# Block-diagonals of B by a select on GpSimd from a ScalarE copy, in place of products on VectorE

## The reference

```python
x = conv(in_proj(ctx)); u = silu(x + conv_b)          # 256 channels, 256 tokens
dt_low, Bm, Cm = split(x_proj(u), [8, 8 + 16])        # Bm, Cm: 16 states per token
d = softplus(dt_proj(dt_low) + dt_proj_b)
def step(state, inp):                                 # d, b, c, u of one token
    state = state * exp(d[..., None] * A) + (d * u)[..., None] * b[:, None, :]
    return state, einsum('bdn,bn->bd', state, c)
y = (scan(step) + D * u) * silu(layernorm(x_in))
x = x_in + tanh(g_xattn) * y
out = x + tanh(g_ffn) * ffn(layernorm(x))             # quantized up, relu^2 gate, rmsnorm, quantized down
```

## Time and profile before

| | us |
|---|---|
| device time, median of 3 runs | 235.77 (234.69 to 237.27) |
| device time of the profiled execution | 236.09 |
| span of the profiled execution, first to last instruction | 234.3 |
| PE busy | 208.6 (89%) |
| DVE busy | 201.1 (86%) |
| POOL busy | 141.0 (60%) |
| ACT busy | 139.2 (59%) |

### The profile page before, as it was taken

How to read it: one execution, slowest core, us unless ns; L and a number is a source line. 1 busy time by engine, 2 the same in 40 slices (tenths; PEclk the granted TensorE clock), 3 DMA queues, 4 the chain that set the end, 5 groups by cost and what they waited for, 6 DMA issues and landing times.

```text
span 234.3 us, 3448 instructions
## 1 busy us (share of the span) xinstructions
PE 208.6 (89%) x1142; PEld 164.8 (70%) x1142; DVE 201.1 (86%) x299; ACT 139.2 (59%) x352; POOL 141.0 (60%) x98
## 2 busy tenths in 40 slices
...
DMA packets 9808, 14.01 MB, mean 60 GB/s; under 512 B 2520, under 2 KB 7360, under 8 KB 9792
## 3 DMA queue, kind: packets, MB, share of 16 engines
...
## 4 chain that ended last, share of the span: by engine, by line
PE 65%; DVE 23%; issue 6%; POOL 2%; ACT 2%; DVEq 0%; POOLq 0%
PE m_ps L910 20%; PE y_ps L932 17%; PE w_ps L961 10%; DVE bd L674 5%; PE w_ps L978 4%; DVE hb L729 3%; POOL hb L354 2%; PE w_ps L863 2%; DVE xc L658 2%; PE y_ps L832 2%; PE w_ps L879 1%; PE w_ps L987 1%; PE w_ps L871 1%; PE w_ps L885 1%; DVE xn L753 1%
## 5 line engine op out<-in xcount | busy, mean ns | idle before, releaser
L354 POOL TENSOR_TENSOR hb<-hb,cs 128x1024 f32<-128x1024 f32 x31 | 73.9, 2395 | 27.5 <-DVE hb L729 26.9
L729 DVE TENSOR_TENSOR_SCAN hb<-dA,m_ps 128x1024 f32<-128x1024 f32 x32 | 72.5, 2278 | 6.2 <-PE m_ps L910 5.5
L562 ACT ACTIVATE dA<-dt,nega 128x255 f32<-128x255 f32 (+1 forms) x160 | 59.4, 455 | 17.2 <-DVE hb L729 10.3
L910 PE MATMUL m_ps<-bd,duT 128*128 128x256 f32 (+1 forms) x224 | 63.9, 433 | 4.5 <-issue 3.8
L932 PE MATMUL y_ps<-hb,identf 128*128 128x256 f32 (+1 forms) x320 | 59.6, 339 | 0.7 <-POOL hb L354 0.6
L932 PEld LDWEIGHTS y_ps<-hb,identf 128*128 128x128 f32 x320 | 51.0, 191 | 6.7 <-POOL hb L354 1.4
L910 PEld LDWEIGHTS m_ps<-bd,duT 128*128 128x128 f32 x224 | 44.0, 202 | 16.5 <-issue 9.5
L961 PE MATMUL w_ps<-w13T,xqT 128*128 128x352 bf16 x192 | 30.6, 313 | 0.6 <-ACT xqT L583 0.5
L961 PEld LDWEIGHTS w_ps<-w13T,xqT 128*128 128x128 bf16 x192 | 18.5, 98 | 11.8 <-issue 1.6
L588 ACT ACTIVATE ru<-w_ps,finv 128x352 f32<-128x352 f32 x16 | 8.8, 548 | 20.3 <-PE w_ps L961 20.3
L674 DVE TENSOR_TENSOR bd<-identf,w_ps 128x1024 f32<-128x1024 f32 x16 | 18.7, 1213 | 1.4 <-PE w_ps L885 1.4
...
## 6 DMA issues: line engine op xcount, KB each, us to landing
...
```

The costliest lines, as they stand in the source:

```text
L354: E.tensor_tensor(h_g, h_g, cs[:, s0:s0 + sn, l0:l0 + ln], ALU.mult).then_inc(hc_end if (b, i, h) == OUT_END else hc_ok[h], 1)
L562: last = act_fn(dA_g[:, s, 1:ln], dt[:, p, h, l0 + 1:l0 + ln], ACT.Exp, scale=nega[:, h, s0 + s:s0 + s + 1])
L729: V.tensor_tensor_scan(hb[:, k % 3, h], dA[:, k % 2, h].rearrange("p n l -> p (n l)"), m_ps[:, h], 0.0, ALU.mult, ALU.add).then_inc(scan_o ...
L910: last = T.matmul(m_q[:, :, c * P - l0:(c + 1) * P - l0], duT[:, p, c, h * P:(h + 1) * P], bd[:, r, c, n0 + sn // 2 * q:n0 + sn // 2 * (q ...
```

## The change

A new step `bts` on ACT copies the transposed B (128 x 32) from PSUM to SBUF, once for each batch. The step `bd` moves from DVE to POOL, where two `affine_select` instructions read that copy, spread over 128 columns with stride 0, and keep it on the diagonal. PE makes one `bT` for each batch instead of two (four in all are gone: `bT/0.1`, `1.1`, `2.1`, `3.1`). `mix` waits for `bd_ok` alone. `relu` gets one wait more, for the `iqT` of two batches before.

```diff
@@ FILLS
-    "bT": [("bd", "dve")], "duT": [("duT", "act")],
+    "bT": [("bts", "act")], "duT": [("duT", "act")],
@@ build
         bd = sb("bd", [P, 2, HALVES, NS // 2, P])
+        bts = sb("bts", [P, 2, HALVES, NS])
@@ gpsimd
+                elif name == "bd":
+                    pool.wait_ge(free["act"], emptied("bT", b, 0))
+                    if b:
+                        pool.wait_ge(m_full, HALVES * (NG * (b - 1) + NG // 2 * (i + 1)))
+                    for c in range(HALVES):
+                        nc.gpsimd.affine_select(
+                            out=bd[:, i, c], in_=bts[:, p, c, NS // 2 * i:NS // 2 * (i + 1)].unsqueeze(2)
+                            .broadcast_to([P, NS // 2, P]), compare_op=ALU.is_equal, fill=0.0, base=0,
+                            pattern=[[0, NS // 2], [-1, P]], channel_multiplier=1).then_inc(bd_ok, 1)
@@ scalar
+                elif name == "bts":
+                    act.wait_ge(work_full, full("bT", b, 0))
+                    if b >= 2:
+                        act.wait_ge(bd_ok, 2 * HALVES * (b - 1))
+                    act_fn(bts[:, p].rearrange("p c n -> p (c n)"), bank("bT", b, 0)[:, 0:HALVES * NS],
+                           ACT.Copy).then_inc(free["act"], 1)
                 elif name == "relu":
                     h, c = i // 2, i % 2
                     act.wait_ge(work_full, full("up", b, i, 0))
+                    if b >= 2:
+                        act.wait_ge(work_full, full("iqT", b - 2, h, 1))
@@ vector
-                elif name == "bd":
-                    dve.wait_ge(work_full, full("bT", b, i))
-                    if b:
-                        dve.wait_ge(m_full, HALVES * (NG * (b - 1) + NG // 2 * (i + 1)))
-                    for c in range(HALVES):
-                        V.tensor_tensor(bd[:, i, c], identf[:, :].unsqueeze(1).broadcast_to([P, NS // 2, P]),
-                                        bank("bT", b, i)[:, c * NS + NS // 2 * i:c * NS + NS // 2 * (i + 1)]
-                                        .unsqueeze(2).broadcast_to([P, NS // 2, P]),
-                                        ALU.mult).then_inc(free["dve"] if c == HALVES - 1 else bd_ok, 1)
@@ tensor
-                        if c < HALVES - 1:
-                            pe.wait_ge(bd_ok, 2 * b + r + 1)
-                        else:
-                            pe.wait_ge(free["dve"], emptied("bT", b, r))
+                        pe.wait_ge(bd_ok, HALVES * (2 * b + r) + c + 1)
```

The orders of PE, ACT, DVE and POOL in `PLAN` are all written anew; two lines of it (POOL's first):

```diff
-        w_res/0.0 w_res/0.1 w_res/0.2 w_lo/0.0 w_lo/0.1 diag/0.0 w_lo/0.2 cubic/0.0 w_res/0.3 dtadd/0.0 w_lo/0.3
...
+        w_res/0.0 w_res/0.1 w_lo/0.0 w_lo/0.1 diag/0.0 w_res/0.2 bd/0.0 w_lo/0.2 bd/0.1 w_res/0.3 z/0.0 cubic/0.0
...
```

More of the change, by code:

```diff
@@ L53 @@
-        sum1/1.1 dtproj/2.0 bT/2.0 xqT/0.0 mix0/1.3 mix1/1.3 up/0.0 bT/2.1 sum0/1.2 sum1/1.2 duT/2.0 sum0/1.3
-        mix0/2.0 sum1/1.3 mix1/2.0 yT/1.0 skip/2.0 mix0/2.1 up/0.1 mix1/2.1 mix0/2.2 sum0/2.0 sum1/2.0 mix1/2.2
-        up/0.2 sum0/2.1 sum1/2.1 up/0.3 mix0/2.3 mix1/2.3 xqT/1.0 xdbl/3.0 up/1.0 dtproj/3.0 bT/3.0 bT/3.1 sum0/2.2
-        sum1/2.2 sum0/2.3 sum1/2.3 up/1.1 duT/3.0 up/1.2 mix0/3.0 up/1.3 mix1/3.0 mix0/3.1 iqT/0.0 yT/2.0 skip/3.0
-        sum0/3.0 mix1/3.1 down/0.0 mix0/3.2 sum1/3.0 sum0/3.1 iqT/0.1 sum1/3.1 xqT/2.0 mix1/3.2 down/0.1 mix0/3.3
@@ L58 @@
-        up/2.0 iqT/1.0 up/2.1 up/2.2 up/2.3 mix1/3.3 skip/3.1 yT/3.0 iqT/1.1 sum0/3.2 sum1/3.2 down/1.0 down/1.1
-        sum0/3.3 xqT/3.0 sum1/3.3 up/3.0 up/3.1 iqT/2.0 yT/3.1 iqT/2.1 down/2.0 down/2.1 xqT/3.1 up/3.2 up/3.3
-        iqT/3.0 down/3.0 iqT/3.1 down/3.1
+        warm/0.0 ctxT/0.0 winT/0.0 inproj/0.0 xpwT/0.0 dtwT/0.0 warm/0.1 w/0.0 w/0.1 w/0.2 ctxT/1.0 xdbl/0.0 bT/0.0
+        w/0.3 inproj/1.0 w/0.4 w/0.5 skip/0.0 dtproj/0.0 w/0.6 ctxT/2.0 ctxT/3.0 inproj/2.0 xdbl/1.0 duT/0.0
+        dtproj/1.0 bT/1.0 mix0/0.0 mix1/0.0 w/0.7 mix0/0.1 inproj/3.0 mix1/0.1 mix0/0.2 sum0/0.0 sum1/0.0 sum0/0.1
```

78 lines of the change are left out of this document (41 added, 37 removed).

## The result

The changed kernel takes 244.0 us (median of 4 runs, 242.57 to 245.41), the kernel before beside it 235.6: a ratio of 1.033 (95% interval 1.027 to 1.039), slower by 8.4 us. Forecast were 234.4 us with a range up to 239.5. The prediction was wrong, in its sign too. The profiled execution took 245.41 us (span 243.7). Some executions of a kernel are a few per cent slower at a lower granted clock of PE, and the ratios leave them out.

A forecast was written before the change was run, and what follows sets the result against it. The prediction took PE to bound most of the middle, after a latency-bound start. Its terms, 7.3 - 4.7 - 1.9 - 2.4 = -1.7 us, took the span from 234.3 to 232.6, giving 234.4 us profiled, with an 8-in-10 range of 230.5 to 239.5.

The forecast's parts named there:

- at 77% that is 1.8 us more for DVE: Middle: a busier POOL slows DVE's subtractions and normalizations by 1.8 us, covered by DVE's 14 us, so no cost.
- 4.7: Behind the first scan: PE's remaining work is shorter by 4.7 us, 3.2 done earlier and 1.5 from three `bT` gone.
- rival 4: Middle: DVE was the bound there, so PE's kept stalls vanish too; 228.7, or 229 to 231.5 us; chance 0.22.
- The middle, -1.9: Batch 1: of PE's 5.6 us lost, 3.7 us of stall stay since most scans come ahead of `x1/0.0`; -1.9 us.
- The start, +7.3: Before the first scan: POOL's longer queue delays `du/0.0` and `z/2.0`; first scan near 46.1 instead of 38.8, +7.3 us.
- The first `mix` is ready by then: Start: `duT` copied by 42, then 3.8 us for `mix` at half clock, ready by the first scan near 46.1.
- a gain of 3.2: Start: PE does `w/0.5`, `w/0.6`, `xdbl/1.0`, `dtproj/1.0` and `bT/1.0` ahead of the first `mix`; -3.2 us.
- The end, -2.4: After the last `up`: moved `down` and `iqT` steps fill PE's gaps, including 1.73 us ahead of the last `iqT`; -2.4 us.
- a select at 1.10 us: POOL: a 128 x 1024 select costs 1.1 us, range 1.65 and 2.4; all 16 add 17.6 us.
- the first scan after 49: Start: sign against the forecast, which falls if the first scan starts before 43 or after 49 us.
- Rival 2: POOL's queue: the select is dear; 238.2 us at 1.65 us a select, near 243.5 at 2.4; chance 0.25.
- Rival 3: Start lost, nothing comes back: later gains become stalls behind POOL's selects, only 7.3 - 4.7 counts; 238.7 us; chance 0.13.

The follow-up runs named there:

- e4: The changed kernel with the 12 selects of batches 1 to 3 replaced by one-column memsets, orders and waits kept: 236.7 us, ratio 1.001.
- e12: The changed kernel with the 12 selects of batches 1 to 3 moved later in POOL's order, nothing else changed: 238.5 us, ratio 1.011.
- e5: The kernel before with DVE's `bd` products of batches 1 to 3 replaced by one-column memsets on DVE: 236.06 us, ratio 1.000.
- e7: The changed kernel with only `z/2.0` moved on DVE, from ahead of the first scan to behind `scan0/0.2`: 245.3 us, ratio 1.039.
- e14: e12 with batch 0's selects also moved back on POOL, behind `du/0.0` and `w_res/0.4`: 239.0 us, ratio 1.013.
- e8: The kernel before with both `down/2` steps moved behind the last `up` on PE, and their final steps on DVE moved too: 243.4 us, ratio 1.032.

## Why the prediction was wrong, point by point

- **The step that failed** is "at 77% that is 1.8 us more for DVE. DVE has 14 us to cover it with, so nothing". It spread the lock evenly over POOL's share of busy time and then paid for it with an average of DVE's free time. What counts is which DVE instruction stands beside which select: they stood beside `cubic`, `dt`, `x1`, `quant1` and the small steps of `outscale`, which are on DVE's way to the next batch's `dt` and scans. Those instructions are 7.1 us longer than in e4, the total is 7.3 us longer, and about 5 of these go with the placement alone (e12: 1.033 to 1.011).
- **The sum again.** The forecast had 7.3 for the start and -9.0 (4.7, 1.9 and 2.4) from the first scan to the end: a span of 232.6. Measured were 11.4 and -2.0: 243.7. Without the 12 selects the second term is -10.5 (e4). So the miss of 11.1 us is 4.1 at the start and 8.5 for the selects (by the profiles; 7.3 by the medians), less 1.5 that the order gave beyond its forecast.
- **What DVE sheds is worth nothing** (e5). The forecast counted nothing for it in its sum, rightly, but rival 4 gave it up to 6 us and a chance of 0.22. The products filled DVE's waits for ScalarE, and part of DVE's 164.5 busy us in the middle was waiting that the record counts as work.
- **The middle, -1.9**: from the first to the end of the last scan the change gained 3.0 us, where 6.6 were forecast (4.7 of PE work moved ahead or gone, and this term). The new order by itself gains 11.4 us there (e4); 3.1 of these are PE's work that now stands behind the last scan. That more scans come ahead of `x1/0.0` is my reason for the rest; no run tested it. The selects took 8.4 of them (157.0 us from first to last scan instead of 148.6).
- **The start, +7.3**: it was +11.4. `du/0.0` (40.6 for 39.0) and `z/2.0` (46.6 for 46.1) were near. The step that failed is "The first `mix` is ready by then": it began at 46.3 and ended at 50.1. POOL's queue made `du/0.0` 8.5 us late (forecast 6.9), ScalarE's order added 0.8 up to the copy of `duT`, and PE another 2.1, since `inproj/2.0`, `dtproj/1.0` and `bT/1.0` with their waits for `w_hi/0.6` and `conv/2.0` stood ahead of `mix`. The forecast had put such steps of PE down as a gain of 3.2 and asked nowhere when PE would be through with them. `z/2.0` was not the last wait (e7), but it was the next one: it set the first scan in e14. The 3.8 us for that `mix` held (3.76).
- **The end, -2.4**: this term nearly held. The gap of 1.73 us ahead of the last `iqT` is gone (none above 0.34 from the last `up` on), and behind the last scan PE stands idle for 4.0 us instead of 6.0. The tail is no shorter for it, 36.5 us instead of 35.5, since PE does 3.1 us more work in it (32.5 us instead of 29.5) that stood ahead of the last scan before. On the old order `down/2` alone could not be moved so (e8): it filled one gap and was missing in another.
- **What held**: a select at 1.10 us, with the fixed part taken from the 8-element row; four `bT` less on PE. Of the signs that it named against itself, the first scan after 49 came true.
- **Rival 2** gave 243.5 at its dear end, near the result, by a cause that did not happen. **Rival 3** (the start is lost and nothing comes back, 238.7) had the sign and a wrong mechanism: the order gave back nearly all of the start (e4), and the selects took it.
